# A four-layer attention and feed-forward kernel: the first attention's turned bias is loaded earlier in the queue of loads

## What is computed

```
q, k, v = LN(x) @ Wq.T + bq,  ctx @ Wk.T + bk,  ctx @ Wv.T + bv      (16 heads)
logits  = scale * q @ k.T + dist * f(distance_scaling)               (128 queries x 120 keys, a head)
x       = x + softmax(logits) @ v @ Wo.T + bo
```

## Time and profile before

| | us |
|---|---|
| median of 3 runs | 3376.16 |
| lowest and highest of the runs | 3375.64, 3383.22 |
| the profiled execution's own time | 3387.81 |
| its span, first to last instruction | 3385.8 |
| PE busy | 2735.7 (81%) |
| VectorE busy | 2155.1 (64%) |
| ScalarE busy | 1558.6 (46%) |
| GpSimd busy | 738.3 (22%) |

### The profile page before, as it was taken

How to read it: one execution, slowest core, us unless ns; L and a number is a source line. 1 busy time by engine, 2 the same in 40 slices (tenths; PEclk the granted TensorE clock), 3 DMA queues, 4 the chain that set the end, 5 groups by cost and what they waited for, 6 DMA issues and landing times.

```text
span 3385.8 us, 123504 instructions
## 1 busy us (share of the span) xinstructions
PE 2735.7 (81%) x46829; PEld 1890.6 (56%) x46829; DVE 2155.1 (64%) x6318; ACT 1558.6 (46%) x3530; POOL 738.3 (22%) x999
## 2 busy tenths in 40 slices
PE   2888887599998998899989699995599994319994
PEld 1666665477775444677754366663366663207773
DVE  5666666877776777677772477777677775612223
ACT  3444445355554333555554155556555553303331
POOL 1222230033331000000000233331000001764553
PEclk9999997599998999899989799997699995559997
DMA  7222234022223000000000011112200002112214
GB/s 207 70 68 70 68 72 153 16 48 51 51 51 122 1 0 0 16 10 10 10 7 0 9 22 20 20 20 60 66 21 21 22 22 66 52 42 72 65 44 161
DMA packets 247825, 161.41 MB, mean 48 GB/s; under 512 B 135893, under 2 KB 221819, under 8 KB 246663
## 3 DMA queue, kind: packets, MB, share of 16 engines
q1 hardware_dynamic: 238470, 145.67, 16.8%
q0 software_dynamic: 9216, 13.88, 1.2%
HBM read 107.89 MB, written 56.82 MB: 49 GB/s over the span
## 4 chain that ended last, share of the span: by engine, by line
PE 54%; DVE 17%; issue 11%; SPq 6%; DMA 5%; POOL 4%; ACT 2%; ACTq 0%; DVEq 0%; POOLq 0%
PE ps L585 8%; PE ps L524 6%; DVE negmax L1306 6%; PE ps L730 5%; PE ps L533 5%; PE ps L862 4%; PE ps L852 4%; DMA ffb<-b_dram 4%; POOL slots L1838 3%; PE ps L605 3%; PE ps L571 3%; PE ps L506 3%; DVE qk L1340 2%; SPq L361 2%; PE ps L600 2%
## 5 line engine op out<-in xcount | busy, mean ns | idle before, releaser
L1306 DVE TENSOR_REDUCE negmax<-ps 128x4 f32<-128x480 f32 (+1 forms) x1280 | 790.3, 659 | 324.4 <-PE ps L533 308.0
L940 ACT ACTIVATE ex<-ps 120x1024 f32<-120x1024 f32 (+1 forms) x640 | 659.9, 1033 | 240.0 <-PE ps L571 239.9
L1789 POOL TENSOR_SCALAR ffb<-ffb 128x480 bf16<-128x480 int32 (+1 forms) x128 | 232.5, 1816 | 619.9 <-PE ps L571 478.0
L561 PE MATMUL ps<-qk 32*120 32x128 f32 (+1 forms) x10240 | 362.2, 280 | 0.0
L585 PE MATMUL ps<-ex,vpad 120*32 120x128 f32 (+1 forms) x10240 | 355.1, 280 | 2.3 <-issue 1.4
L925 ACT COPY mT<-ps 128x128 bf16<-128x128 bf16 x320 | 85.2, 266 | 583.2 <-PE ps L539 583.2
L561 PEld LDWEIGHTS ps<-qk 32*120 32x120 f32 (+1 forms) x10240 | 316.7, 186 | 0.0
L585 PEld LDWEIGHTS ps<-ex,vpad 120*32 120x32 f32 (+1 forms) x10240 | 265.9, 111 | 57.3 <-issue 53.8
L1838 POOL DMA_INDIRECT slots<-xw,slot_of x128 | 132.1, 1032 | 582.4 <-DVEq L1684 540.9
L533 PE MATMUL ps<-qk 32*128 32x480 bf16 (+1 forms) x1280 | 252.8, 389 | 2.3 <-DVE qk L1287 1.7
L1287 DVE SCALAR_TENSOR_TENSOR qk<-ps,cols,cpack 128x480 f32<-128x480 f32 (+1 forms) x320 | 228.7, 715 | 40.0 <-ACT qk L919 40.0
(11 more groups left out here) (242 smaller groups left out, 5065.1 us busy)
## 6 DMA issues: line engine op xcount, KB each, us to landing
ffb<-b_dram SPq DMA_DIRECT2D x256, 90.0 KB, 2.4
ctxT<-in_ctxT SPq DMA_DIRECT2D x256, 60.0 KB, 1.8
ffb<-in_mask SPq DMA_DIRECT2D x256, 60.0 KB, 2.0
slots<-xw SPq DMA_DIRECT2D x1, 10560.0 KB, 31.0
h_all<-slots SPq DMA_DIRECT2D x40, 264.0 KB, 2.8
z<-xw SPq DMA_DIRECT2D x1, 8192.0 KB, 24.5
b_dram<-bparts SPq DMA_DIRECT2D x64, 90.0 KB, 1.9
w_sb<-in_L_W SPq DMA_DIRECT2D x2, 2048.0 KB, 10.2
```

The costliest lines, as they stand in the source:

```text
L561: pe.matmul(bank(g)[:, k * P:(k + 1) * P], kblk[of, j, k * nk:(k + 1) * nk], qs[of, j, :], start=False, stop=False, skip_group_check=True)
L940: act.activation(ex[0:nk, j, c * 1024:(c + 1) * 1024], b_ps[c][0:nk, :], ACT.Exp).then_inc(S["e_ready"], 1)
L1306: dve.tensor_reduce(negmax[:, j, HG * g:HG * g + HG], a_ps[g % 2][:, 0:HG * nk].rearrange("p (a n) -> p a n", a=HG), AX.X, ALU.max, negate ...
L1789: pool.tensor_scalar(mask4[:, j, :, :].rearrange("p c n -> p (c n)"), raw[:, j, :, :].rearrange("p c n -> p (c n)"), 0.0, MASKED, ALU.is_e ...
```

## The change

In the first attention, SP's pass for I begins with `bias_back` of I+2, which used to be its end: it now stands ahead of `reload` of I+1 and `bias_out` of I+3. Its wait before it overwrites the buffer is another: a new semaphore, `b4_read`, which PE raises with the last of the 48 bias matmuls of `scores_by_key`, in place of `b_ready`. The wait for the store is kept. The other attentions and all other engines are as they were.

```diff
                 def bias_back(I, used):
                     t, j = I
                     if used:
-                        sp.wait_ge(S["b_ready"], nth("b_ready", s, num(I) - 2))
+                        sp.wait_ge(S["b4_read"], nth("b4_read", s, num(I) - 2))
                         sp.sem_inc(S["sp_step"], 1)
                     sp.wait_ge(S[f"b_out{j}"], nth_dma("b_out0", s, t))
                     for r in range(4):
...
                 def body(I, has):
+                    if s == 0 and has(2):
+                        bias_back(item(I, 2), True)
                     if has(3):
                         reload(item(I, 1))
-                    if s == 0:
-                        if has(3):
-                            bias_out(item(I, 3))
-                        if has(2):
-                            bias_back(item(I, 2), True)
+                    if s == 0 and has(3):
+                        bias_out(item(I, 3))
                     if has(-2) and s == 4:
                         store_y(item(I, -2))
...
-                                pe.matmul(mine, bias4(j, part)[of, m, :], bc(identb[of, of], HG),
-                                          start=part == 0 and m == 0, stop=False, skip_group_check=True)
+                                mm = pe.matmul(mine, bias4(j, part)[of, m, :], bc(identb[of, of], HG),
+                                               start=part == 0 and m == 0, stop=False, skip_group_check=True)
+                    if s == 0:
+                        mm.then_inc(S["b4_read"], 1)
```

More of the change, by code:

```diff
@@ L193, in build @@
         z = nc.dram_tensor("z", [NZ, P], F32, kind="Internal").ap()
-        names = """consts_in weights_in stage_w_in u_out ctx_in0 ctx_in1 bias_in0 bias_in1 pe_step b_out0 b_out1 b4_in0 b4_in1 u_in0 u_in1
+        names = """consts_in weights_in stage_w_in u_out ctx_in0 ctx_in1 bias_in0 bias_in1 pe_step b_out0 b_out1 b4_in0 b4_in1 b4_read u_in0 u_in1
             y_out0 y_out1 y_in0 y_in1 y_in2 y_in3 moe_w_in out_done stage_go sq_in sq_out dve_step setup_dve setup_pe
@@ L209, in build @@
         USES.update({n: [1, 3] for n in ("bias_in0", "bias_in1")})
-        USES.update({n: [0] for n in ("bln_ready", "biasf_ready", "bleft_ready", "bias2_ready", "bias3_ready", "b_out0", "b4_in0")})
+        USES.update({n: [0] for n in ("bln_ready", "biasf_ready", "bleft_ready", "bias2_ready", "bias3_ready", "b_out0", "b4_in0", "b4_read")})
         USES.update({n: [3] for n in ("eps_ready",)})
```

## The result

The changed kernel takes 3302.27 us (median of four runs, 3299.52 to 3303.01), the kernel before 3376.41 beside it (3375.64 to 3383.22). The ratio is 0.9769, with a 95% interval of 0.9753 to 0.9785: 2.3% faster. The profiled execution took 3302.31 us, 85.5 less than that of before. In the experiments some move by a few more; the tile names tell which they are.

The account below looks back on a forecast made before the run. PE's wait for the turned bias, in a ring through SP's queue, was taken to bound the first attention; 60.5 us of waits plus 15.9 of clock give 76.4, so 3311.4 or 3299.8, middle 3306 us, range 3295 to 3325.

Parts of the forecast that it names:

- The ring: First attention: PE's L506 releases SP's context, store and bias loads, which PE's next L524 awaits; this sets the 7.24 us turn.
- The waits of the moved loads: On SP, the last L556 matmul and the earlier store's landing both end near 303.4, so loads start 5.3 us earlier.
- The margin of 3 to 4.5 us: Time between the landing of the last moved bias load, 307.3 or 308.7, and PE's want of it at 311.8.
- The length of a turn: First attention: 6.25 us a turn without the wait, from readings of 6.17 and 6.24; 61 turns take 381.3 us.
- The new increment: The semaphore increment on the last L556 matmul, 64 of them, was taken to cost 0.
- The estimate of 26 ns: Increments queue at the end of packed matmuls, about 26 ns each; 64 would make the sum 1.7 us smaller.
- The clock: First attention: drops of PE's granted clock go with its waits; the rival that they stay had chance 0.08.
- The term of 15.9 us: First attention, 61 turns: 457.66 - 60.5 - 381.3 = 15.9 us, put down to the lower clock and expected back.
- that rival: VectorE takes over: PE waits 0.4 us for L1340 in all 61 turns, 24 us lost again, gain 52; chance 0.07.
- SP as the bound: SP's queue becomes the ring, 4.86 us, deciding from a 3.8 us landing, slower than before from 5.1; chance 0.03.
- The sum: A gain of 76.4 us: 3311.4 from the profiled execution, 3299.8 from the median, 3306 taken.
- The middle of the two starting points: 3306 us, between 3311.4 and 3299.8, as the place of the 11.65 us between profiled execution and median was open.

Follow-up runs that it names:

- Half of the order: The kernel before, with only the store of the bias moved behind the loads of the turned bias on SP: 3321.29 us, ratio 0.9828.
- the new wait alone: The kernel before, in its old order on SP, with the loads waiting for b4_read in place of b_ready: 3378.37 us, ratio 0.9997.
- the idle time put in: The changed kernel, with PE made to wait ahead of the first half of the scores by query for an unneeded GpSimd step: 3366.99 us.
- seven stores: The changed kernel with seven more small stores on SP's queue per pass, between context load and bias store: 3448.08 us, ratio 1.0189.
- 0.24 us less of PE's work: The changed kernel without the third bf16 part of the bias in the scores by key, 32 small matmuls not 48: 3298.83 us, ratio 0.9748.
- three stores: The changed kernel with three more small stores on SP's queue per pass, between context load and bias store: 3317.08 us, ratio 0.9816.
- the order alone: The changed kernel with the old wait, b_ready in place of b4_read: 3306.38 us, ratio 0.9783.

## Why the prediction was right

*The ring.* Right in each step. Half of the order took the store's issue out of it, 0.69 us, and the turn at full clock shortened by 0.77; the whole order took the wait away; the new wait alone did nothing. What the prediction did not say is that the new semaphore is hardly needed: with the old one the loads of a regular turn still land over a microsecond early.

*The waits of the moved loads.* Both were forecast to end within 0.1 us of each other, near the end of L556. The trace after has the store landed at 311.80 and L555 done at 312.18, with the loads 0.18 us behind. The margin of 3 to 4.5 us is 3.6 by the trace: the fourth load leaves at about 313.7, lands a median of 2.2 us later, 315.9, and is read at 319.51.

*The length of a turn.* 6.25 was taken, 6.17 and 6.24 were the readings, and the mean is 6.22: 6.17 regularly, which is the turn without a wait in the earlier trace rows, and 6.40 once in four. The new increment costs nothing that the trace shows, since the turn with it is as long as the one without it, 6.17. The estimate of 26 ns from the Trainium skill, "TensorE: Matmul & The Clock Gate", "The cost: per-tile semaphore tail", is not seen here: there it stands for increments behind one another, here a long run of matmuls follows one.

*The clock.* The term of 15.9 us was inferred, as what the waits and the forecast turn left over. 78.5 us were won in the 61 turns and 60.5 of them are waits; the other 18.0 are this term and the 2.1 by which the turns came out shorter than 61 x 6.25. The granted clock gives the same size: 0.96 over 433.56 us is some 17 us short of full speed. The start gave 1.6 more, which the sum had not counted: from item 0 to item 2 the clock was 0.90 before and is 1.00 now. The experiments stand on either side. With half of the order, waits of at most 0.7 us, 7.5 us in all, and no drops from 100 to 470 us. With the idle time put in, about 1.0 us in every turn with the transfers of the changed kernel, and drops as before. With seven stores, waits of 79.3 us in all and a clock of 0.87. So idle time is enough to bring the drops, and no late load is needed for it. This agrees with the Trainium skill, the same page, "HAM oscillation — how this bites in real kernels", by which waits of PE are paid a second time in clock; the waits in its example are 3 to 5 us, which the prediction did not say, so that for waits of about 1 us it is the runs here that decide. Where a drop falls is not settled: with much the same wait in every turn, from three to seven places in sixty turns are hit (three with the idle time put in, five before, seven with the new wait alone).

*The rivals.* PE waits for VectorE in one turn of four, which is that rival in small and costs 0.23 x 15 = 3.5 us; with 0.24 us less of PE's work it waits in every second turn, so little is left. SP as the bound was worked out with 4.86 us for its ring, and measures 4.47: the landing is 1.76 and not 2.42 (207.91 to 209.67 with three stores), and some 0.39 from the loads to the context had been left out. So SP had 1.7 us to spare and not 1.39. Its way of failing was right: loaded with 3.9 us more, the same order is slower than the kernel before. A landing of over 3.8 us, which the prediction named as its condition, came up in the run with the order alone (4.04), and there PE waited.

*The sum.* From the profiled execution, 3387.81 - 76.4 = 3311.4 was forecast, and 3302.31 came, because 85.5 us went: 81.8 by the end of the stage, 5.4 more than the terms above, and 3.6 in the second attention, whose clock was low for a shorter time (0.79 against 0.73 in its first 60 us, 0.91 against 0.87 in its last 40). From the medians, 74.1 us went against 76.4. The middle of the two starting points, 3306, was 4 us high. By the profiled executions the terms of the sum were 5.4 us short, by the medians 2.3 too large, so it is partly luck that the median came to lie only 2.5 us from 3299.8. Where the 11.65 us sat by which the profiled execution of before lay above the median is not shown, since no execution of that kernel at its median was profiled.

## What to carry to other kernels

A wait that recurs in every turn, with issue and flight of a load in the chain, is a ring: look for the first thing in it that need not be there, here a load queued behind another's wait, and move it; what releases its buffer matters only if it comes later than the queue. Idle time of TensorE in a stage that is otherwise full costs more than its length, as its clock may fall after it; about 1 us in a turn of 7 cost a fifth to a quarter more here, and shorter, rarer waits cost nothing more. Before a queue that issues in order is given a wait for something just begun, add up its own turn, landing included, and see that it stays below the engine's that it feeds.

## What was not expected

Each small store added to SP's queue cost 0.55 to 0.59 us of its turn, though the issue itself shows 0.33 to 0.36; the rest lies between the issues. In the program each of them takes its address from the loop's counter; whether that is what takes the time was not tried.

Runs of the kernel before scatter by 17.5 us (3373.39 to 3390.89 in the sixteen beside the first experiments), those of the changed one by 3.5 and 9.5 us (four and five). It is tempting to put this down to the waits and their drops, but the runs do not show it. The changed kernel with idle time put in has both and scatters by 6.0 us in seven runs; and the profiled execution of the kernel with the new wait alone, at 3396.33 us 8.5 longer than that of before, has 61 turns of 457.2 us in all, no longer than the 457.66 of before, so that difference lies elsewhere.
